# A graph network's edge logits: one accumulating pick per tile instead of three wide operations per five tiles, and one selection moved from ScalarE to VectorE

## What is computed

```python
h = x @ W
a_src = h @ att_src
a_dst = h @ att_dst
...
alpha = a_src[src] + a_dst[dst] + a_edge
alpha = jax.nn.leaky_relu(alpha, negative_slope=0.2)
amax = jax.ops.segment_max(alpha, dst, num_segments=N)
...
ex = jnp.exp(alpha - amax[dst])
denom = jax.ops.segment_sum(ex, dst, num_segments=N)
w = ex / (denom[dst] + 1e-16)
out = jax.ops.segment_sum(h[src] * w[:, None], dst, num_segments=N)
```

## Time and profile before

| | us |
|---|---|
| median of 3 runs (7795.66 to 7801.17) | 7800.38 |
| the profiled execution | 7800.69 |
| its span, first to last instruction | 7798.9 |
| PE busy | 5942.3 |
| POOL busy | 5236.8 |
| DVE busy | 2566.9 |
| ACT busy | 1011.1 |

### The profile page before, as it was taken

One profiled execution on the slowest core, in us unless ns is written; L12 is line 12 of the kernel. 1 busy time (PEld: TensorE's weight loads), 2 busy tenths in 40 slices (PEclk: granted clock), 3 DMA queues, 4 the chain that ended last, 5 costly groups with the idle time before them and its releaser, 6 DMA issues.

```text
span 7798.9 us, 99480 instructions
## 1 busy us (share of the span) xinstructions
PE 5942.3 (76%) x24625; PEld 4370.6 (56%) x24626; DVE 2566.9 (33%) x8202; ACT 1011.1 (13%) x2795; POOL 5236.8 (67%) x5030
## 2 busy tenths in 40 slices
PE   2378886776662788888887999997888888885555
PEld 1267774333331456667776666665666576663333
DVE  6733334555555222222223333332222122222222
ACT  2500001222221100000000111111111100000000
POOL 2067776888883677767776555554777677767777
PEclk6555555555555555556766555556888766665555
DMA  4632224555556222233332222223444444432222
GB/s 132 177 96 61 62 62 79 79 79 79 79 79 162 74 59 59 59 92 113 114 113 79 77 82 82 81 82 118 152 158 157 133 128 131 129 113 58 58 58 57
DMA packets 514928, 749.68 MB, mean 96 GB/s; under 512 B 113089, under 2 KB 366385, under 8 KB 503959
## 3 DMA queue, kind: packets, MB, share of 16 engines
q0 software_dynamic: 260160, 450.93, 24.2%
q1 hardware_dynamic: 254664, 297.72, 11.9%
HBM read 543.93 MB, written 204.60 MB: 96 GB/s over the span
## 4 chain that ended last, share of the span: by engine, by line
POOL 32%; PE 28%; issue 17%; DMA 15%; DVE 4%; SPq 1%; ACT 1%; POOLq 0%; DVEq 0%; ACTq 0%
POOL ring L724 25%; PE PS L1710 11%; POOL part L738 7%; PE PS L1760 6%; DMA part<-ring,cur 5%; PE PS L1717 4%; DMA ring<-tab_l,SRC 3%; DMA ring<-tab_l3a,SRC 2%; DMA ring<-tab_l2a,SRC 1%; PE PS L1712 1%; PE PS L1750 1%; DMA SCR<-hi_d 1%; SPq L483 1%; DMA ring<-tab_l2b,SRC 1%; DVE SCR L1458 1%
## 5 line engine op out<-in xcount | busy, mean ns | idle before, releaser
L1710 PE MATMUL PS<-QSEL,ring 128*128 128x64 f32 x12500 | 2956.2, 373 | 822.9 <-DMA ring<-tab_l3c,SRC 336.3
L1710 PEld LDWEIGHTS PS<-QSEL,ring 128*128 128x128 f32 x12500 | 2520.1, 272 | 1550.2 <-issue 629.7
L738 POOL DMA_INDIRECT part<-ring,cur x625 | 977.3, 1564 | 237.1 <-issue 153.5
L724 POOL DMA_INDIRECT ring<-tab_l2c,SRC x625 | 602.6, 964 | 505.8 <-PE PS L1717 303.3
L724 POOL DMA_INDIRECT ring<-tab_l,SRC x625 | 599.5, 959 | 438.1 <-issue 399.3
L1760 PE MATMUL PS<-X,SCR 128*128 128x512 f32 x1280 | 845.6, 786 | 0.0
L724 POOL DMA_INDIRECT ring<-tab_l2a,SRC x625 | 596.2, 954 | 334.9 <-issue 313.5
L724 POOL DMA_INDIRECT ring<-tab_l3a,SRC x625 | 600.7, 961 | 255.0 <-issue 238.9
L1791 PE MATMUL PS<-ring,SCR 32*128 32x128 f32 x1250 | 494.5, 497 | 350.6 <-ACT SCR L868 350.6
L724 POOL DMA_INDIRECT ring<-tab_l3b,SRC x625 | 600.5, 961 | 230.6 <-issue 223.6
L724 POOL DMA_INDIRECT ring<-tab_l3c,SRC x625 | 606.2, 970 | 215.1 <-issue 214.5
(11 more groups left out here) (303 smaller groups left out, 5302.8 us busy)
## 6 DMA issues: line engine op xcount, KB each, us to landing
tab_l3a<-SCR SPq DMA_DIRECT2D x40, 1024.0 KB
tab_l3b<-SCR SPq DMA_DIRECT2D x40, 1024.0 KB
SCR<-in_src SPq DMA_DIRECT2D x125, 320.0 KB, 3.7
SCR<-part SPq DMA_DIRECT2D x100, 256.0 KB, 3.8
part<-zeros SPq DMA_DIRECT2D x9, 2624.0 KB, 21.6
tab_l3c<-SCR SPq DMA_DIRECT2D x40, 512.0 KB
SCR<-hi_d SPq DMA_DIRECT2D x125, 160.0 KB, 3.0
ACC_B<-in_edge_attr SPq DMA_DIRECT2D x5, 2000.0 KB
```

Source lines behind the costliest of these rows:

```text
L724: pool.indirect_dma_start(ring[:, slot, 0:width], None, tab[p][:, :], bass.IndirectOffsetOnAxis(SRC[:, t:t + 1], 0)).then_inc(sem(f"row{sl ...
L738: pool.indirect_dma_start(part_d[s][:, :], bass.IndirectOffsetOnAxis(cur[:, s:s + 1], 0), ring[:, s, 0:D], None, compute_op=ALU.add).then_ ...
L1710: ins = mm(PS[:, s, ch * QWIN:(ch + 1) * QWIN], ring[:, slot, ch * P:(ch + 1) * P], hot, start=e == 0 and ch == 0, stop=e == end, skip_gro ...
```

## The change

`low_digits` and `products` go. `pick` becomes five SCALAR_TENSOR_TENSOR operations per chunk, one for each tile: compare the ramp of 40 with the tile's low digit (a pointer scalar in `SLO`), multiply with the tile's 40 columns in PSUM, and sum them by the accumulator into one column of `ASRC`. The stagger goes with the other two, so `pick` of chunk q waits for the matmuls of q (`src_mm`) itself. Chunk 4's selection moves from ACT to DVE (`BY_DVE = (1, 3, 4)`), so ACT makes chunks 0 and 2, with the semaphores' counts changed on SP, ACT and TensorE. DVE makes selection 1 ahead of picks 0, selection 3 ahead of picks 1 and selection 4 ahead of picks 2; in the first turn all three come ahead of the picks.

```diff
--- before.py
+++ after.py
@@ -260,6 +260,8 @@
                 for u in range(2):
                     body(i, u)
 
+        BY_DVE = (1, 3, 4)
+
         def following(i, u):
 
             if isinstance(i, int) and 2 * i + u + 1 == GROUPS:
@@ -470,8 +472,10 @@
                 hi_chunk(0, s)
             with sp.Fori(1, 25) as i:
                 for s in range(5):
-                    hots = 2 * i if s % 2 else 3 * i
-                    sp.wait_ge(sem("hot_dve" if s % 2 else "hot_made"), hots - (2 if s % 2 else 3) + s // 2 + 1)
+                    if s in BY_DVE:
+                        sp.wait_ge(sem("hot_dve"), 3 * i - 3 + BY_DVE.index(s) + 1)
+                    else:
+                        sp.wait_ge(sem("hot_made"), 2 * i - 2 + s // 2 + 1)
                     sp.sem_inc(sem("turn"), 1)
                     hi_chunk(i, s)
 
@@ -831,16 +835,14 @@
 
             def hot(i, s):
 
-                act.wait_ge(sem("hot_abs"), 3 * i + s // 2 + 1)
+                act.wait_ge(sem("hot_abs"), 2 * i + s // 2 + 1)
                 nc.scalar.activation(hot_hi[:, s, :], hot_hi[:, s, :], ACT.Relu, bias=ones[0:HI, 0:1], scale=-1.0).then_inc(sem("hot_made"), 1)
 
             def hots(i):
                 distance(i, 0)
                 distance(i, 2)
                 hot(i, 0)
-                distance(i, 4)
                 hot(i, 2)
-                hot(i, 4)
             act.wait_ge(sem("const"), 10)
             hots(0)
             with act.Fori(1, 25) as i:
@@ -1209,20 +1211,13 @@
 
 
 
-            def low_digits(q, s):
-                if not isinstance(q, int) or q >= 5:
-                    dve.wait_ge(sem("picked"), q - 4)
-                vec.tensor_tensor(picks[:, s], iotaL[:, 0:LO].unsqueeze(1).to_broadcast([P, 5, LO]),
-                                  cols(SLO, q, 5).unsqueeze(2).to_broadcast([P, 5, LO]), ALU.is_equal).then_inc(sem("pick_hot"), 1)
-
-            def products(q, s):
-                dve.wait_ge(sem("pick_hot"), q + 1)
+            def pick(q, s):
                 dve.wait_ge(sem("src_mm"), q + 1)
-                vec.tensor_tensor(picks[:, s], picks[:, s], PS[:, s, 0:5 * LO].rearrange("p (j l) -> p j l", l=LO), ALU.mult).then_inc(sem("pick_mul"), 1)
-
-            def pick(q, s):
-                dve.wait_ge(sem("pick_mul"), q + 1)
-                vec.tensor_reduce(cols(ASRC, q, 5), picks[:, s], AX, ALU.add).then_inc(sem("picked"), 1)
+                dve.sem_inc(sem("turn"), 1)
+                for j in range(5):
+                    ins = vec.scalar_tensor_tensor(picks[:, s, j, :], iotaL[:, 0:LO], SLO[:, bass.ds(q * 5 + j, 1)], PS[:, s, j * LO:(j + 1) * LO],
+                                                   ALU.is_equal, ALU.mult, accum_out=ASRC[:, bass.ds(q * 5 + j, 1)])
+                ins.then_inc(sem("picked"), 1)
 
 
             def hot(i, s):
@@ -1234,22 +1229,15 @@
                     dve.sem_inc(sem("turn"), 1)
                 vec.tensor_scalar(hot_hi[:, s, :], hi_bc[:, s, :], part[0:HI, :], None, ALU.is_equal).then_inc(sem("hot_dve"), 1)
 
-            low_digits(0, 0)
-            for q in range(5):
-                if q in (0, 1):
-                    hot(0, 2 * q + 1)
-                low_digits(q + 1, (q + 1) % 5)
-                products(q, q)
-                if q:
-                    pick(q - 1, q - 1)
+            for s in BY_DVE:
+                hot(0, s)
+            for s in range(5):
+                pick(s, s)
             with dve.Fori(1, 25) as i:
                 for s in range(5):
-                    if s in (0, 1):
-                        hot(i, 2 * s + 1)
-                    low_digits(5 * i + s + 1, (s + 1) % 5)
-                    products(5 * i + s, s)
-                    pick(5 * i + s - 1, (s - 1) % 5)
-            pick(T // 5 - 1, 4)
+                    if s < 3:
+                        hot(i, BY_DVE[s])
+                    pick(5 * i + s, s)
             km = rounds(dve)
 
             dve.wait_ge(sem("picked"), T // 5)
@@ -1648,10 +1636,10 @@
 
             def rows_of_logits(i, s):
                 q = 5 * i + s
-                if s % 2:
-                    pe.wait_ge(sem("hot_dve"), 2 * i + s // 2 + 1)
+                if s in BY_DVE:
+                    pe.wait_ge(sem("hot_dve"), 3 * i + BY_DVE.index(s) + 1)
                 else:
-                    pe.wait_ge(sem("hot_made"), 3 * i + s // 2 + 1)
+                    pe.wait_ge(sem("hot_made"), 2 * i + s // 2 + 1)
                 if later(i):
                     pe.wait_ge(sem("picked"), q - 4)
                 for j in range(5):
```

## The result

The changed kernel takes 7817.12 us, median of 14 runs (7813.72 to 7828.81); the kernel before, run beside it, takes 7797.53 us (7791.4 to 7807.06). The ratio is 1.0026, with a 95% interval of 1.0018 to 1.0034: slower by 19.6 us. The forecast was 7798, no change that could be measured. The time lies inside the range of 7791 to 7824, on the far side of it, and in the rival "the sequencer sets the turn", which had been given +14 to +25.

The account below looks back on a forecast made before the run. The loop was taken as bound by ACT, SP and `hi_d` landings, its last `hi_d` DMA setting the end. A turn of 6.5 against 6.62 over 23 turns gives −2.8, plus 0.9: −2 us, 7798, range 7791 to 7824.

Parts of the forecast that it names:

- the sequencer sets the turn: Rival: DVE's address computations and unhidden waits set the loop's turn, 7.2 to 7.7 us, +14 to +25; chance 0.19 including both late.
- what carries a change to the end: Behind the loop: SP's last `hi_d` DMA sets the end, 97 us of DMA follow; DVE has some 20 us slack.
- ACT's half: Loop on ACT and SP: ACT loses one of three chunks, period 6.28 us against 6.45; −4 us if DVE keeps up.
- only another order could give −18 us: SP's order in the loop: only chunk 2 issued straight after its Relu, 5.7 us a turn, would give −18 us.
- the engine's price of a pick: DVE engine in the loop: 0.175 us with a free read, 0.025 taken for the read, 0.20 per pick, 5.9 a turn.
- The rival of unhidden reads: DVE engine in the loop: accumulator reads aren't hidden, 0.255 a pick, turn 7.25 us, 0 to +15 us; chance 0.22.
- the sum for DVE's sequencer: DVE's queue per turn: 4.2 us for 25 picks, 1.8 for small instructions, 0.2 for the loop's turn, 6.2 us.
- W: DVE's work per turn, the larger of engine and sequencer: likeliest 6.2 us; above 6.54 it is the loop's period.
- The signs named for it: On DVE in the loop: no idle time for TensorE, ACT waiting for matmuls instead, gaps put down to issue.
- The alternative in the prediction: DVE's queue: a pick's two addresses computed by two instructions, 0.21 us a pick and 7.2 a turn.
- L1420 with its step of 0.264: DVE row with one computed address each, said to keep to its engine's need; taken as evidence against the sequencer rival.
- the 0.9 of the last chunk's selection on DVE: Loop's end: the last chunk waits for selection 4, 3.75 us after a Relu 0 instead of 2.9; +0.9 us.

Follow-up runs that it names:

- e5: Kernel before with its three wide operations, only chunk 4's selection moved to DVE; 8801.52 us, ratio 0.9989 to the kernel before.
- e7: Kernel before with chunk 4's selection on DVE and ACT's order changed to Abs 0, Relu 0, Abs 2, Relu 2; 8775.47 us, ratio 0.9961 to before.
- e2: Changed kernel with every turn's picks on the first 25 columns, so no pick computes an address; 8733.50 us, ratio 0.9992 to the kernel before.
- e9: Changed kernel with picks on fixed columns and ACT's order Abs 0, Relu 0, Abs 2, Relu 2; 8768.82 us, ratio 0.9953 to the kernel before.
- e4: Changed kernel with the picks' accumulator output dropped, so no read and one address fewer; 8735.51 us, ratio 0.9999 to the kernel before.
- e6: Changed kernel without the five increments per turn of semaphore turn ahead of the picks; 8809.20 us, ratio 1.0001 to the kernel before.

## Why the prediction was wrong

**Right: what carries a change to the end.** The last `hi_d` chunk moved by 20.15 us and the first gather by 19.88, the zeroing between them stayed at 97 us, DVE's slack behind the loop was never used up, and the program's median followed with 19.6.

**Right: ACT's half.** The forecast was 6.28 plus 0.15 a turn and −4 us; e5 measured 6.42 and −4.0 at the gather. The remark that only another order could give −18 us was right in its direction; e7 gave −30, with a turn of 5.17 where 5.7 had been worked out.

**Right: the engine's price of a pick, and better than taken.** Worked out was 0.175 with a free read; with 0.025 for the read I took 0.20. The engine's own step is 0.177 (first turn, e2 and e9). Its need was put at 5.9 a turn and is 5.32. The rival of unhidden reads falls. So does the price of about 75 ns per instruction that the Trainium skill gives (Vector Engine (DVE) Microarchitecture Reference, Measured stream behaviour on trn2), where it is laid on the read: no run here shows it; a read costs at most 0.01. The agreement of 0.20 in the loop was thus by accident: the right number, made by the queue and not by the read.

**The step that failed: the sum for DVE's sequencer.** It gave W = 6.2 as the likeliest; measured is 7.465. The mechanism had been named, as a rival with a chance of 0.19, and the formula told what to do with W; the sizes were too small, in three terms. The signs named for it came too: next to no wait of the picks for TensorE, and gaps put down to issue.

| term of W | forecast us | measured us | shown by |
|---|---|---|---|
| address computation for a pick | 0.053 to 0.080 | 0.093 | 558 FUSED_REGOPS at L1218 |
| gap and hand-offs round it | 0.08 | 0.105 | step 0.198 less 0.093 |
| 25 picks | 4.2 | 4.95 | 25 × 0.198 |
| waits, marks, selections, branch | 2.0 | 2.5 | 7.465 − 4.95 |

The row of L1225 and L1215 is a row of *other* address computations. That of a pick covers two operands, the pointer scalar and the accumulator's output, in one instruction of 93 ns; that of e4, with one operand, takes 57. And the small instructions, put at 0.06, cost up to 0.095 each (e6). The 0.06, the 0.02 of a hand-off and the 0.2 of the branch were not read from rows of such instructions, and no run shows them. The kernel before had such rows, in ACT's queue, where a small instruction and the issue behind it take 0.08:

```profile
255.17 0.02 ACTq L826
255.19 0.06 issue
255.24 0.04 ACTq L828
255.28 0.04 issue
```

The alternative in the prediction, two instructions at 0.21 a pick, is not what happened (it is one, and the step is 0.198), but its W of 7.2 to 7.7 holds the 7.465.

The worse fault lies behind the sizes. L1420 with its step of 0.264 was read as evidence against a bound by the queue. But a 128x128 operation of 0.26 covers any queue step up to 0.26; it could say nothing about a queue step of 0.198 under an operation that needs 0.177. The sum for the sequencer was 6.2 against an engine's 5.9, and the one gap in it with a row was SP's. With sums that near each other and terms counted some 55 times a turn, a miss of 0.02 in each is a microsecond. From W = 6.54 on the period is W itself, and so it came: 7.465 − 6.61 over the 22 steady turns is 18.8, and the 0.9 of the last chunk's selection on DVE, which the prediction had, makes 19.7, against 20.15 found.

**Open.** What the 0.105 beside the address computation and the 0.07 behind a mark consist of is not split further by any run; the chain calls it issue. No run changes the waits, the branch or the selections' own addresses alone, so their share of the 2.5 us is not shown either. The start, where the picks waited 2.5 us for TensorE in the first looped turn, lies in the 20.15 and was not looked into.

## What to carry to other kernels

Before splitting a wide operation into many narrow ones in a loop, count what the engine's queue must do for each, at its full price: here 0.198 us for a pick with its computed addresses and 0.095 for a mark. Set that against what the operation itself needs, here 0.177, for only that can cover it. A busy share below one says nothing against such a bound. Its sign is idle time put down to "issue", or of one length whoever it is put down to, and its test is the same code with constant addresses. And where the work around a buffer changes, look again at the order in which it is held: one exchange of two lines on ACT brought the first gather forward by 26.6 us (e7 against e5), where the moved selection alone brought 4.0 (e5) and the edit with its addresses free 3.7 (e2).

## What the runs showed that was not expected

A DVE_READ_ACCUMULATOR of 0.08 starts together with the next operation and costs its engine almost nothing: the picks stand 0.177 apart with it and 0.168 without. On DVE's queue the computation of two addresses took 0.093 and of one 0.057, and a mark on a semaphore that shows as 0.02 took 0.095 from a loop bound by the queue. A loop of DVE, written out for 24 turns, was 0.9 us a turn faster than as a loop, and still no faster than the kernel before: its chain then runs through the `hi_d` transfers, SP and ACT, as in the kernel before.
